# Cross-attention of a decoder layer: maxima transposed into another PSUM bank, tasks spread anew over the slots, context loaded behind the key copies, and the values' bias moved

## The reference

```python
q = _w8a8_linear(x, wq, bq)            # x and wq rounded to 8 bits, product scaled back
k = cond @ wk.T + bk;  v = cond @ wv.T + bv
scores = einsum('bhnd,bhld->bhnl', q, k) * inv_sqrt_d + mask[:, None]
attn = softmax(scores, axis=-1)
o = einsum('bhnl,bhld->bhnd', attn, v)
return _w8a8_linear(o, wo, bo)         # o rounded to 8 bits by rows again
```

## Time and profile before

| | us |
|---|---|
| median of three runs | 4096.11 |
| profiled execution, first to last instruction | 4114.0 |
| profiled execution as timed | 4115.7 |
| TensorE matmuls busy | 3691.4 (90%) |
| VectorE busy | 2596.5 (63%) |
| ScalarE busy | 1596.1 (39%) |
| GpSimd busy | 648.8 (16%) |

### The profile page before, as it was taken

How to read it: one execution, slowest core, us unless ns; L and a number is a source line. 1 busy time by engine, 2 the same in 40 slices (tenths; PEclk the granted TensorE clock), 3 DMA queues, 4 the chain that set the end, 5 groups by cost and what they waited for, 6 DMA issues and landing times. The chain is left out here.

```text
span 4114.0 us, 95372 instructions
## 1 busy us (share of the span) xinstructions
PE 3691.4 (90%) x34364; PEld 2671.0 (65%) x34364; DVE 2596.5 (63%) x6225; ACT 1596.1 (39%) x2842; POOL 648.8 (16%) x784
## 2 busy tenths in 40 slices
PE   7999999994899989989898998899899859999998
PEld 6988999993556655655655555565565636666665
DVE  4444444444677767767777777677777756666665
ACT  3222223221344544444444444444445433332322
POOL 0000000003011111101111011111111103332222
PEclk9999999997899999999999999899999979999999
DMA  2000000003546454654646555364554520000000
GB/s 94 13 13 12 9 7 8 12 9 76 95 90 106 90 103 84 109 94 82 108 80 111 91 97 101 73 113 89 95 102 93 93 60 5 13 12 17 15 12 13
DMA packets 121819, 256.97 MB, mean 62 GB/s; under 512 B 18564, under 2 KB 99276, under 8 KB 118364
## 3 DMA queue, kind: packets, MB, share of 16 engines
q1 hardware_dynamic: 113136, 243.95, 31.5%
q10 hardware_dynamic: 8300, 7.69, 0.7%
HBM read 99.79 MB, written 9.83 MB: 27 GB/s over the span
## 5 line engine op out<-in xcount | busy, mean ns | idle before, releaser
L1391 DVE CUSTOM_DVE_ANT_0 ca_rowmax<-ca_rowmax,ca_msk 100x1024 f32<-100x1024 f32 (+1 forms) x1024 | 929.2, 921 | 383.6 <-PE ca_rowmax L1159 377.1
L1097 ACT ACTIVATE ca_prob<-ca_unit 128x800 f32<-128x800 f32 x640 | 534.6, 835 | 558.7 <-PE ca_unit L1283 558.6
L1159 PE MATMUL ca_rowmax<-ca_ks,ca_qs 96*100 96x512 bf16 (+1 forms) x1536 | 518.6, 408 | 81.0 <-DMA ca_ks<-ca_ks 47.6
L1283 PEld LDWEIGHTS ca_unit<-ca_qs,ca_ks 99*128 99x128 bf16 (+1 forms) x6144 | 356.0, 100 | 212.2 <-issue 124.8
L1002 POOL TENSOR_TENSOR ca_key_part<-ca_key_rest,ca_key_part 128x512 bf16<-128x512 f32 (+1 forms) x192 | 211.5, 1102 | 1680.3 <-ACT ca_key_part L1064 1680.3
L1246 PE MATMUL ca_acc<-ca_prob,ca_vaug 128*17 128x100 f32 x12288 | 444.6, 258 | 21.1 <-issue 20.8
L1283 PE MATMUL ca_unit<-ca_qs,ca_ks 99*128 99x100 bf16 (+1 forms) x6144 | 439.4, 212 | 24.1 <-issue 15.3
L1141 PE MATMUL ca_ring<-ca_wvT,ca_ctxT 128*128 128x256 f32 (+1 forms) x1536 | 418.2, 419 | 0.9 <-ACT ca_qs L1075 0.6
L1141 PEld LDWEIGHTS ca_ring<-ca_wvT,ca_ctxT 128*128 128x128 f32 (+1 forms) x1536 | 314.9, 207 | 79.7 <-issue 17.8
L1132 PE MATMUL ca_ring<-ca_ctxT,ca_wkT 128*128 128x512 f32 (+1 forms) x768 | 346.1, 573 | 2.3 <-ACT ca_ctxT L1048 2.3
L1159 PEld LDWEIGHTS ca_rowmax<-ca_ks,ca_qs 96*100 96x100 bf16 x1536 | 154.7, 128 | 243.8 <-issue 173.1
...
## 6 DMA issues: line engine op xcount, KB each, us to landing
ca_ks<-ca_key_part SPq DMA_DIRECT2D x768, 90.2 KB, 4.1
...
```

Source lines behind the costliest of these rows:

```text
L1097: act.activation(prob[:, s, :], unit[:, :, 0:QUAD * N], ACT.Exp).then_inc(bc.freed[0], 1)
L1159: last = pe.matmul(rowmax[0:N, s0:s1], qs[0:STACK, par, h, :], ks[0:STACK, par, h, s0:s1], start=True, stop=True)
L1283: return pe.matmul(unit[0:rows(t0 + k), k, j * N:(j + 1) * N], ks[:, par, h, keys(k)], qs[:, par, h, :], start=(j == 0), stop=True, skip_g ...
L1391: dve.tensor_tensor_reduce(rowmax[0:N, s0:s1], rowmax[0:N, s0:s1], msk[:, par, s0:s1], 1.0, -3.0e38, ALU.add, ALU.max, top[:, bank, h:h + ...
```

## The change

- `mr` transposes the parts of the maxima into the third bank of `rowmax` instead of `unit`; it now stands in the order of `ml`, and ScalarE copies from there.
- The tasks are spread over the slots anew.
- SP waits for the last `ct` and loads the next context behind the last puts, ahead of the second repeat, instead of ahead of all the copies.
- ScalarE copies the values out of the ring without their bias; VectorE adds the bias to the mean in `eo` (one more link in its chain: O_STEPS 9, O_HALF 7). As the weights of the softmax add up to one, the mean then has the same bias.
- exp of the last pair is one instruction over both tiles, with the unused rows of the second in it.

```diff
-        1: [("eo",), ("kp", 0, 0)],
-        2: [("mh", 7), ("kp", 0, 1), ("km", 0, 0)],
-        3: [("ml", 7), ("ct", 1, 0), ("ct", 1, 1), ("ex",), ("km", 0, 1)],
-        4: [("mh", 8), ("kp", 1, 0), ("ml", 8), ("ey",)],
-        5: [("mr", 1), ("mh", 9), ("kp", 1, 1), ("km", 1, 0)],
-        6: [("ml", 9), ("ct", 2, 0), ("ct", 2, 1), ("km", 1, 1), ("ez",)],
-        7: [("mh", 10), ("kp", 2, 0), ("ml", 10)],
-        8: [("mh", 11), ("kp", 2, 1), ("km", 2, 0)],
-        9: [("ml", 11), ("vp", 0), ("km", 2, 1)],
-        10: [("mh", 12), ("qq",), ("ml", 12)],
-        11: [("mr", 2), ("qx",), ("mh", 13), ("vp", 1), ("qp",)],
-        12: [("ml", 13)],
-        13: [("mh", 14), ("vp", 2), ("ml", 14), ("qs", 0)],
-        14: [("mh", 15), ("qs", 1), ("ma",)],
-        15: [("ml", 15), ("vp", 3)],
-        16: [("mh", 0), ("ml", 0)],
-        17: [("mr", 3), ("mh", 1), ("vp", 4), ("mf",)],
-        18: [("ml", 1)],
-        19: [("mh", 2), ("ml", 2)],
-        20: [("mh", 3), ("vp", 5)],
-        21: [("ml", 3)],
-        22: [("mh", 4), ("ml", 4)],
-        23: [("mr", 0), ("mh", 5)],
-        24: [("ml", 5)],
+        1: [("eo",), ("kp", 0, 0), ("mh", 7)],
+        2: [("ml", 7), ("kp", 0, 1), ("km", 0, 0), ("ct", 1, 0), ("ct", 1, 1)],
+        3: [("ex",), ("mh", 8), ("kp", 1, 0), ("km", 0, 1)],
+        4: [("ml", 8), ("ey",), ("kp", 1, 1), ("km", 1, 0), ("ct", 2, 0), ("ct", 2, 1)],
+        5: [("mr", 1), ("mh", 9), ("kp", 2, 0), ("km", 1, 1)],
+        6: [("ml", 9), ("kp", 2, 1), ("km", 2, 0), ("mh", 10), ("ez",)],
+        7: [("ml", 10), ("vp", 0), ("km", 2, 1)],
+        8: [("mh", 11), ("ml", 11), ("qq",)],
+        9: [("vp", 1), ("mh", 12)],
+        10: [("ml", 12), ("qx",), ("mh", 13)],
+        11: [("mr", 2), ("vp", 2), ("qp",), ("ml", 13)],
+        12: [("mh", 14), ("ml", 14)],
+        13: [("vp", 3), ("mh", 15)],
+        14: [("ml", 15), ("qs", 0), ("qs", 1), ("ma",)],
+        15: [("vp", 4)],
+        16: [("mr", 3), ("mh", 0), ("ml", 0)],
+        17: [("mh", 1), ("mf",)],
+        18: [("ml", 1), ("mh", 2)],
+        19: [("ml", 2), ("mh", 3)],
+        20: [("ml", 3), ("vp", 5)],
+        21: [("mh", 4), ("ml", 4)],
+        22: [("mr", 0), ("mh", 5)],
+        23: [("ml", 5)],
+        24: [],
...
-    cur_order = [t for t in timeline if t[0] in ("u", "mr")]
-    top_order = [t for t in timeline if t[0] in ("mh", "ml", "eo", "ex", "ey")]
+    cur_order = [t for t in timeline if t[0] == "u"]
+    top_order = [t for t in timeline if t[0] in ("mh", "ml", "mr", "eo", "ex", "ey")]
...
-        bm = Banks(nc, sems, "ca_top", top_order, lambda t: int(t[0] == "ml"),
+        bm = Banks(nc, sems, "ca_top", top_order, lambda t: int(t[0] in ("ml", "mr")),
...
                 put(1, (0,))
                 repeat(0)
                 put(1, (1, 2))
+                if more:
+
+                    bn.wait_full(sp, ("ct", 2, C - 1), b)
+                    sp.sem_inc(sp_passed, 1)
+                    load_ctx(b + 1)
                 repeat(1)
...
+                elif task[0] == "vp":
...
+                        return act.activation(
+                            vaug[0:r, par, t + n0:t + n1, :, 0:DH],
+                            ring[bank][0:r, n0 * D:n1 * D].rearrange("p (t h d) -> p t h d", t=n1 - n0, h=H), ACT.Copy)
...
-                                   unit[STACK:FULL, 0, :].bitcast(BF16)[:, 0:QUAD * N], ACT.Copy)\
-                        .then_inc(bc.freed[bank], 1)
+                                   rowmax[STACK:FULL, 2 * 512:3 * 512].bitcast(BF16)[:, 0:QUAD * N], ACT.Copy)\
+                        .then_inc(bm.freed[bm.bank(task)], 1)
...
+                act.activation(prob[:, 2 * (p % 2):2 * (p % 2) + 2, :], unit[:, :, 0:QUAD * N], ACT.Exp)\
+                    .then_inc(bc.freed[0], 1)
...
+                    chain.link(dve.tensor_tensor(o, o, bias_row[0:N, 1, :], ALU.add))
```

More of the change, by code:

```diff
@@ L869, in load_ctx, with stack @@
                     .then_inc(ctx_loaded, 16)
-            def stack(b, par):
+            def stack(b, par, more):
                 def put(half, parts):
@@ L904, in step @@
                 first = isinstance(b, int) and b < 2
-                if more:
-                    bn.wait_full(sp, ("ct", 2, C - 1), b)
-                    sp.sem_inc(sp_passed, 1)
-                    load_ctx(b + 1)
-                stack(b, par)
+                stack(b, par, more)
                 if more:
@@ L1065, in do_task, with v_out @@
                         .then_inc(mid_out, 1)
+                elif task[0] == "vp":
+                    bank = bn.bank(task)
+                    bn.wait_full(act, task, b)
+                    t = 2 * task[1]
+                    def v_out(r, n0, n1):
+                        return act.activation(
+                            vaug[0:r, par, t + n0:t + n1, :, 0:DH],
+                            ring[bank][0:r, n0 * D:n1 * D].rearrange("p (t h d) -> p t h d", t=n1 - n0, h=H), ACT.Copy)
+                    if rows(t + 1) == TL:
+                        v_out(TL, 0, 2).then_inc(bn.freed[bank], 1)
+                    else:
+                        v_out(TL, 0, 1)
+                        v_out(last_rows, 1, 2).then_inc(bn.freed[bank], 1)
                 elif task[0] == "qx":
@@ L1079, in do_task @@
                     h0 = task[1] * QUAD
[L1080 to L1081 removed]
+                    bm.wait_full(act, task, b)
                     act.activation(qs[STACK:FULL, par, h0:h0 + QUAD, :].rearrange("p h n -> p (h n)"),
[L1083 to L1084 removed]
+                                   rowmax[STACK:FULL, 2 * 512:3 * 512].bitcast(BF16)[:, 0:QUAD * N], ACT.Copy)\
+                        .then_inc(bm.freed[bm.bank(task)], 1)
                 elif task[0] == "ex":
@@ L1163, in do_task @@
                 if kind == "mr":
-                    g, bank = task[1], bc.bank(task)
-                    bc.wait_empty(pe, task, b)
+                    g = task[1]
+                    bm.wait_empty(pe, task, b)
                     pe.wait_ge(top_done, NQ * b + g + 1)
                     for j in range(QUAD):
-                        last = pe.transpose(unit[STACK:FULL, bank, :].bitcast(BF16)[:, j * N:(j + 1) * N],
+                        last = pe.transpose(rowmax[STACK:FULL, 2 * 512:3 * 512].bitcast(BF16)[:, j * N:(j + 1) * N],
                                             top_part[:, g * QUAD + j, :], ident_b[0:N, 0:N])
-                    last.then_inc(bc.filled[bank], 1)
+                    last.then_inc(bm.filled[bm.bank(task)], 1)
                     return
@@ L1359, in do_task @@
                     dve.tensor_tensor(qry[:], qry[:], bias_row[0:N, 0, :], ALU.add).then_inc(qry_done, 1)
-                elif kind == "vp":
-                    bank = bn.bank(task)
-                    bn.wait_full(dve, task, b)
-                    t = 2 * task[1]
-                    def v_out(r, n0, n1):
-                        return dve.tensor_tensor(
-                            vaug[0:r, par, t + n0:t + n1, :, 0:DH],
-                            ring[bank][0:r, n0 * D:n1 * D].rearrange("p (t h d) -> p t h d", t=n1 - n0, h=H),
-                            bias_row[0:r, 1, :].rearrange("p (h d) -> p h d", h=H).unsqueeze(1)
-                            .broadcast_to([r, n1 - n0, H, DH]), ALU.add)
-                    if rows(t + 1) == TL:
-                        v_out(TL, 0, 2).then_inc(bn.freed[bank], 1)
-                    else:
-                        v_out(TL, 0, 1)
-                        v_out(last_rows, 1, 2).then_inc(bn.freed[bank], 1)
                 elif kind == "ma":
```

15 lines of the change are left out of this document (3 added, 12 removed).

## The result

The changed kernel takes **4213.3 us** (median of four runs, 4194.23 to 4216.75) where the kernel before takes 4098.74 on the same chips: **1.0266 times as long, 95% interval 1.0237 to 1.0295**. The forecast was 4152, with a range that ended at 4212. The sign and the place were right; the rise is 115 us instead of 56.

The account below looks back on a forecast made before the run. TensorE's order of work plus its waits bound the kernel. Waits of 8.5 us a turn go and 9.8 come (+1.3), or +2.3 with the lock; the middle, 31 x 1.8 = 56 us, on the median 4096 gives 4152 us, range 4062 to 4212.

Parts of the forecast that it names:

- (a): At "mr": the transposes no longer need the scores' bank, so their wait for exp goes, 2.75 us a turn.
- (b): At "mh" 0: the wait for copied keys goes, 1.3 us a turn, by earlier key product and later context.
- (c): Old slots 12, 18 and 21: too little filling to cover exp, waits of 0.33 us each, 1.0 in all, removed.
- (d): At "qx": the wait for the quantised queries, short by one slot, falls from 1.4 to 0.35 us.
- The ring: Two banks taken in turn: "ct" 1 1 waits 2.0 us for the bank of "kp" 0 1; slot 4 waits 1.8.
- One more lock: Slot 2: GpSimd may hold up VectorE's maxima step, making the wait at "ct" 1 1 up to 3.0 us, not 2.0.
- The clock: TensorE's clock falls about new waits in slots 2 to 4 instead of the DMA wait; its cost taken as unchanged.
- rival (4): Waits and falls add up: locks in each turn and two clock falls instead of one, 4212 us; chance 0.12.
- Median and profile: The profiled execution lasted 0.5% above the median; the rise was added to the median, the difference taken as waits.
- (1): Cross-attention: same added waits, spread so the clock doesn't fall, 4062 us, faster by 0.8%; chance 0.17.
- (2): Slots 1 to 4: VectorE earlier, waits 1.2 and 1.3 us, "mh" 8's gone; 4068 or 4110 us; chance 0.17.
- (3): The key copies, or the context behind them, still come late: 40 us more, 4192 us; chance 0.06.

Follow-up runs that it names:

- e3: The kernel before with only the maxima transposed into the third bank (and "mr" 3 ahead of "mh" 0): 4101.2 us, ratio 1.0018.
- e7: The changed kernel with the next context loaded ahead of the key copies again: 4202.6 us, ratio 1.0269.
- e2: The kernel before with only the next context loaded behind the key copies: 4104.9 us, ratio 1.0007.
- e12: The changed kernel with "km" 0 0 moved behind "ct" 1 1 in slot 2: 4197.7 us, ratio 1.0268.
- e6: The changed kernel with "kp" 0 1 ahead of "ml" 7 in slot 2: 4097.3 us, ratio 1.0014.
- e11: The changed kernel without the values' bias addition on VectorE (its output is another): 4116.1 us, ratio 1.0048.
- e8: The changed kernel with nine unread matmuls ahead of "ct" 1 1 and six ahead of "ct" 2 1 (its output is another): 4141.4 us, ratio 1.0113.
- e10: The kernel before with eight unread matmuls ahead of the wait of "mh" 0 for the copied keys: 4066.7 us, ratio 0.9921.
- e13: e6 with three and five unread matmuls in its two waits at "ct", against e6: 4056.7 us, ratio 0.9916 to the kernel before.

## Why the prediction came out as it did

- **What bounds the kernel.** Right: TensorE's order and its waits. VectorE lost 130 us of work (2596.5 to 2466.1) and it bought nothing.
- **(a) "mr" in the third bank.** The waits for exp went, 2.75 us a turn by the walk. In the new slots this holds, with slot 22's price of 0.8 (measured 33.7 / 29 = 1.2 us). That it is a gain of its own is wrong: in the old slots it is worth nothing (e3).
- **(b) The copied keys.** The wait is gone (40.6 to 0.4 us), and by the new slots, in which "kp" 2 1 is two slots earlier: e7 has them without the move of the context, and no wait for the copies either. The part given to the context is wrong: 22.3 us from puts to "mh" 0 with the context behind them, 22.1 with it ahead (e2), and e7's time equals the changed kernel's.
- **(c), (d) thin slots and "qx".** "qx" waits 0.6 us in all instead of 39.7. "mh" 13 behind "qq" waits 0.86 (0.95 forecast).
- **The ring.** "1.2 us is the least", 2.0 walked, up to 3.0 with the lock: measured 2.77 in 26 turns of 30, 3.0 in three, 2.1 in one. Without the lock it is 1.9 (e12), so the walk of VectorE's queue was right to 0.1 us; with "kp" 0 1 first it is 0.94 (e6), under the "least". Slot 4: 1.8 forecast, 1.39 to 1.85 measured, 1.54 in the mean. "mh" 8 behind "ex": 0.9 forecast, 0.43. The sum of added idle time was +1.8 forecast, +2.05 measured: this term of the sum held. Both totals behind it were too high by 1.2 to 1.4 us a turn (8.5 against 7.1 before; 10.3 against 9.1 after), and that these cancel is partly luck.
- **One more lock.** I left it between yes and no and took the middle. It is there in 26 turns of 31: L1399 at 1.07 us. The Trainium skill (SBUF — State Buffer, section "SBUF: two separate sides") has the rule, which the prediction cites: the one that starts first keeps the other out for its whole length. The trace agrees: 1.07 us, ended with GpSimd's operation. In e11 and e12, where the two don't meet, it is 0.17.
- **The clock: the step that failed.** "I take the clock's cost as unchanged." The term stood at nothing, on the argument that new falls replace old ones. The runs show more falls than before: 56 stretches at 1.2 GHz instead of 39. Of the old ones 17 stood about the wait for the copies, which is gone; of the new ones 50 stand behind two waits a turn, of 2.77 and 1.54 us in slots 2 and 4 (28 and 22 of 30), ahead of key products, which take 3.62 instead of 1.88 us there. The matmuls' busy time rose by 24.6 us in the profiled pair; between the medians the recorded clocks make it some 45 us (an estimate); 72 us go by filling the waits (e8); and e6 and e11 give back about twice the waits they remove (116 us for 54; 97 for 40). Had I priced a second fall in half of the turns, as rival (4) did, the forecast would have been 4152 + 45 = 4197.
- **Median and profile.** The prediction read its rows in an execution 0.5% above the median and added to the median. By the recorded clocks that 0.5% is mostly the clock of the single execution: 0.942 against 0.947. Why the clock differs from one execution to the next is not shown. So 78.5 us of the rise is read in the traces, and the other 36 rests on that estimate.
- **The rivals.** (1) The clock coming back: wrong for the change (0.93), though e8, e10 and e13 show the mechanism. (2) Balance: wrong, VectorE was not earlier; the waits at "ct" are 2.77 and 1.54 us where it had 1.2 and 1.3, and the one at "mh" 8 is still there. (3) wrong. (4), 4212 us: it came out at 4213, and by its mechanism, a lock in most turns and a second fall of the clock; it had a chance of 0.12.

What stays open: how the clock's cost depends on a wait's length. Waits in slot 2 of 0.29 (e13), 0.94 (e6), 1.44 (e11), 1.9 (e12) and 2.77 us (after) stand with clocks of 0.98, 0.96, 0.95, 0.92 and 0.93, with the second wait at 1.4 to 1.9 except in e13. From 1.44 to 1.9 us the falls behind this wait go from 9 to 27 in 30 turns, from 1.9 to 2.77 only to 28. The length alone does not decide it: the wait of 1.5 us in slot 4 has falls in 22 of 30 turns of e11, the one of 1.44 in slot 2 in 9. Why it goes so was not tried.
